# Two blocks of relation products kept in the tail of the row buffer, with nine own rows mixed a stage later

## The chip, the cores and the metric

The kernel runs on one core of a Trainium2 chip. The metric is device time in microseconds (us), the median over runs of the whole kernel. The engines are PE (TensorE: matmuls, with its weight loads shown as PEld), DVE (VectorE), ACT (ScalarE), POOL (GpSimd, which here issues the indirect gathers) and SP (SyncE, which issues plain loads).

## The reference, cut to what matters

A graph of 3125 nodes with 128 features and 53125 edges goes through four layers, each followed by a residual addition and a layer norm: ten steps of propagation, two graph-attention layers, one relational layer and one attention layer. The change lies where the second attention layer ends and the relational layer begins. The relational layer is this:

```python
out = x @ W0
h = jnp.einsum('nd,rdo->rno', x, W)          # 8 relations
msg = h[edge_type, src] * edge_weight[:, None]
out = out + jax.ops.segment_sum(msg, dst, num_segments=num_nodes)
return out / deg[:, None]                     # deg at least 1
```

So each node's row is multiplied by eight matrices (its relation products) and by W0 (its own product). Each edge then fetches one of the eight products of its source node, and the products are summed at the destination.

## The kernel before, in words

Nodes are cut into NB = 25 blocks of 128. Edges are sorted by destination and laid into tiles of 128 slots, CAP = 17 tiles for a block (7 for the last one). Blocks are grouped into seven SETS: 0 to 3, 4 to 7, 8 to 11, 12 to 15, 16 to 19, 20 to 21 and 22 to 24. All engines run one long program and meet only at semaphores; the order on each engine is written out by hand.

Second attention layer (`Layer`, followed by `IntoRelations`). For each block POOL gathers the edges' rows into `t.rows` (a ring of two blocks, 34 slots of 264 floats for each partition). DVE makes one-hot matrices, scores and messages, and PE sums the messages at the nodes. DVE's loop for block b begins with `at_nodes(b - 1)` and goes on with `raise_(b)` and `weigh(b)`, on whose results ACT's exponentials and PE's sums wait, then `messages(b)` and `close(b - 1)`. When a set is closed, DVE normalises it, PE applies `wo`, and DVE adds the result to x and normalises again (`IntoRelations.dve`). Some blocks later, at the places listed in `LATE`, PE multiplies two blocks by the nine relation matrices (L1924), ACT copies the eight relation products of each block to `t.stage` (L2027) and stores them from there to the table `rel_table_b`, and the own product goes to `t.own`.

`t.stage` has STAGES = 7 places, and block b uses place b % 7. DVE also needs the staged products: the loop edge of a node is not gathered but added by `mix(b)`, eight `scalar_tensor_tensor` (L1978) that add to `t.own` each of the eight products times a weight that is zero for all but the node's own relation. Block b + 7 may overwrite a place only when block b is stored (`tabled`) and mixed (`mixed`).

Before the change `MIXED_EARLY = NB - STAGES = 18`: blocks 0 to 17 are mixed inside the second attention layer, at the end of DVE's loop body, by `dve_mix`. Blocks 16 and 17 are mixed at the end of the body for block 22, directly ahead of `at_nodes(22)`. The other seven blocks (18 to 24) are mixed in the next stage, one for each of its first seven blocks. The last set, 22 to 24, has its products made at the very end, by `pe_last`, `act_last` and `dve_last` (L1933 and L1938 on PE, L1957 on ACT, L1970 on DVE, the stores at L1960). POOL waits for all 25 stores before the first gather of the relational layer (`Relations.pool`).

Relational layer (`Relations`). POOL issues 403 gathers (L2611) into `t.rows`, seen as a ring of REL_RING = 4 blocks of 17 rows of 128 floats. DVE makes weighted one-hots for the next block (L2645), mixes, and closes the block (L2651, L2653) when PE has summed it (L2632). After each set the products for the attention layer that follows are made (L2508, L2531, L2560 and the lines after it). Neighbouring blocks share one tile (`shared`, `fetched`): an odd block reads its first tile from the last slot of the even block ahead of it.

Of the kernel before, what the change touches and what calls it, by code (L numbers as in the profile page):

```python
# [16 lines left out]
P = 128  # L17
N = 3125
E = 53125
D = 128  # L20
NB = -(-N // P)
# [15 lines left out]
NREL = 8  # L37
# [6 lines left out]
CAP = 17  # L44
# [18 lines left out]
ALU = mybir.AluOpType  # L63
# [35 lines left out]
class Core:  # L99


    def __init__(self, nc, ctx, dram):
        self.nc, self.ctx, self.dram = nc, ctx, dram
        self.sems = []
# [18 lines left out]
def chained(eng, sem, start=0):  # L123


    count = [start]

    def then(ins):
        count[0] = count[0] + 1
        ins.then_inc(sem, 1)  # L130
        eng.wait_ge(sem, count[0])
    return then
# [1405 lines left out]


STAGES = 7  # L1540


class NormTiles:
# [46 lines left out]
class Tiles:  # L1590


    def __init__(self, c, ctx, y):
        def sb(name, shape, dt=f32):
            return c.sb(ctx, f"t_{name}", shape, dt)
# [29 lines left out]
        fresh = sb("fresh", [P, NB * (SPAN + 1) + 7], bf16)  # L1625
        stage = sb("stage", [P, STAGES, NREL * D])
        weights = sb("weights", [P, 2 * (F + 2 * HEADS)])
# [39 lines left out]
class Enter:  # L1667
# [32 lines left out]
    def pool(self, pool):  # L1700
        self.c.nc.gpsimd.iota(self.t.node[:, :], [[0, 1]], base=0, channel_multiplier=1, allow_small_or_imprecise_dtypes=True).then_inc(self.numbered, 1)
# [122 lines left out]
class IntoLayer:  # L1824
# [38 lines left out]
    def act_late(self, act, i, blocks):  # L1863
        pass
# [4 lines left out]
    def act_last(self, act):  # L1869
        pass  # L1870

    def dve_last(self, dve):
        pass
# [11 lines left out]
class IntoRelations:  # L1885
# [3 lines left out]
    def __init__(self, c, t, table):  # L1889
        self.c, self.t, self.table = c, t, table  # L1890
        self.early, self.late = 0, 0
        self.turned, self.copied, self.done, self.added, self.normed, self.step, self.x_turned, self.x_copied, self.x_done, self.x_out = (
            c.sem(f"into_rel_{n}") for n in ("turned", "copied", "products", "added", "normed", "step", "x_turned", "x_copied", "x_products", "x_out"))
        self.x_out_dve = c.sem("into_rel_x_out_dve")
        self.tabled = [c.sem(f"into_rel_tabled{q}") for q in range(STAGES)]
        self.mixed, self.mix_step = c.sem("into_rel_mixed"), c.sem("into_rel_mix_step")

    def pe(self, pe, layer, i):
        c, t, blocks = self.c, self.t, SETS[i]
# [46 lines left out]
    def act_last(self, act):  # L1946
        c, t, blocks = self.c, self.t, SETS[-1]
        n, k0, m = len(blocks), 3 * blocks[0], len(blocks) * P
        act.wait_ge(self.x_turned, len(SETS))
        act.wait_ge(self.x_done, k0)  # L1950
        c.nc.scalar.copy(t.turned_all[:, 0:m], t.pt[:, 0:m]).then_inc(self.x_copied, 1)
        rows = self.table.rearrange("(r n) f -> n r f", r=NREL)
        for j, b in enumerate(blocks):
            act.wait_ge(self.tabled[b % STAGES], 16 * (b // STAGES))
            act.wait_ge(self.mixed, b - STAGES + 1)
            act.wait_ge(self.x_done, k0 + 2 * j + 1)
            c.nc.scalar.copy(t.stage[:, b % STAGES, 0:4 * D], t.pr[0][:, 0:4 * D]).then_inc(self.x_out, 1)  # L1957
            act.wait_ge(self.x_out, k0 + j + 1)
            act.wait_ge(self.x_out_dve, j + 1)
            act.dma_start(rows[b * P:(b + 1) * P, :, :], t.stage[:, b % STAGES, :].rearrange("p (r f) -> p r f", r=NREL)).then_inc(self.tabled[b % STAGES], 16)  # L1960
        for j, b in enumerate(blocks):
            act.wait_ge(self.x_done, k0 + 2 * n + j + 1)
            c.nc.scalar.copy(t.own[:, b, 0:D], t.pr[j % 2][:, 0:D]).then_inc(self.x_out, 1)

    def dve_last(self, dve):
        t, blocks = self.t, SETS[-1]
        for j, b in enumerate(blocks):
            dve.wait_ge(self.tabled[b % STAGES], 16 * (b // STAGES))
            dve.wait_ge(self.x_done, 3 * blocks[0] + 2 * j + 2)
            self.c.nc.vector.tensor_copy(t.stage[:, b % STAGES, 4 * D:NREL * D], t.pr[1][:, 0:4 * D]).then_inc(self.x_out_dve, 1)  # L1970

    def mix(self, dve, b):

        c, t, v = self.c, self.t, self.c.nc.vector
        then = chained(dve, self.mix_step, b * NREL)
        total = t.own[:, b, 0:D]
        for r in range(NREL):
            last = v.scalar_tensor_tensor(total, t.stage[:, b % STAGES, r * D:(r + 1) * D], t.own_rel[:, r, b:b + 1], total, ALU.mult, ALU.add)  # L1978
            then(last)
        dve.nop().then_inc(self.mixed, 1)  # L1980

    def dve_mix(self, dve, blocks):
        for b in blocks:
            if b < MIXED_EARLY:
                dve.wait_ge(self.x_out, 3 * b + 3)
# [24 lines left out]
    def act_late(self, act, i, blocks):  # L2010
        c, t = self.c, self.t
        if blocks[0] == SETS[i][0]:
            m = len(SETS[i]) * P
            act.wait_ge(self.x_turned, i + 1)
            if i:
                act.wait_ge(self.x_done, 3 * blocks[0])
            c.nc.scalar.copy(t.turned_all[:, 0:m], t.pt[:, 0:m]).then_inc(self.x_copied, 1)
        rows = self.table.rearrange("(r n) f -> n r f", r=NREL)
        for b in blocks:
            if b >= STAGES:  # L2020
                act.wait_ge(self.tabled[b % STAGES], 16 * (b // STAGES))
                act.wait_ge(self.mixed, b - STAGES + 1)
            for n, (lo, hi) in enumerate(REL_PARTS):
                k = 3 * b + n
                act.wait_ge(self.x_done, k + 1)
                to = t.stage[:, b % STAGES, lo * D:hi * D] if n < 2 else t.own[:, b, 0:D]
                c.nc.scalar.copy(to, t.pr[k % 2][:, 0:(hi - lo) * D]).then_inc(self.x_out, 1)  # L2027
            act.wait_ge(self.x_out, 3 * b + 3)
            act.dma_start(rows[b * P:(b + 1) * P, :, :], t.stage[:, b % STAGES, :].rearrange("p (r f) -> p r f", r=NREL)).then_inc(self.tabled[b % STAGES], 16)

    def dve(self, dve, layer, i):
        c, t, blocks, v = self.c, self.t, SETS[i], self.c.nc.vector
# [11 lines left out]
for _i, _blocks in enumerate(SETS):  # L2044
    for _lo in range(0, len(_blocks), 2):
        LATE.setdefault(min(_blocks[-1] + 2 + _lo // 2, NB) if _blocks[-1] < NB - 4 else (NB - 1 if _blocks[-1] < NB - 1 else NB), []).append((_i, _blocks[_lo:_lo + 2]))
MIXED_EARLY = NB - STAGES
REL_PARTS = [(0, 4), (4, NREL), (NREL, NREL + 1)]
NORM_STEPS = 12

# [10 lines left out]
def fetched(b):  # L2061

    return tiles_of(b)[b % 2:]


def shared(b):

    return b % 2 == 0 and b < NB - 1
# [7 lines left out]
def arrived(b):  # L2076

    return 16 * sum(len(fetched(n)) for n in range(b % RING_BLOCKS, b + 1, RING_BLOCKS))
# [19 lines left out]
def slot(k):  # L2098
    return k % (RING_BLOCKS * CAP)
# [475 lines left out]
        last.then_inc(self.split, 1)  # L2575


REL_RING = 4


class Relations:
# [3 lines left out]
    def __init__(self, c, t, table, before, after):  # L2585
        self.c, self.t, self.table, self.before, self.after = c, t, table, before, after
        self.tabled = before.tabled
        self.step, self.hot, self.summed, self.freed, self.normed = (c.sem(f"relations_{n}") for n in ("step", "hot", "summed", "freed", "normed"))
        self.gathered = [c.sem(f"relations_gathered{q}") for q in range(REL_RING)]
        self.rows = t.rows[:, :, :].rearrange("p s f -> p (s f)")[:, 0:REL_RING * CAP * D].rearrange("p (s f) -> p s f", f=D)  # L2590
        self.gathered_last = c.sem("relations_gathered_last")
        self.first_lot = len(tiles_of(NB - 1)) - 2

    def slot(self, k):
        return k % (REL_RING * CAP)

    def arrived(self, b):
        return 16 * sum(len(fetched(n)) for n in range(b % REL_RING, b + 1, REL_RING))

    def pool(self, pool):  # L2600
        c, t = self.c, self.t
        for q, tabled in enumerate(self.tabled):
            pool.wait_ge(tabled, 16 * len(range(q, NB, STAGES)))
        for b in range(NB):
            for k in fetched(b):
                if b >= REL_RING and (k % CAP % SUM_GROUP == 0 or k == fetched(b)[0]):
                    pool.wait_ge(self.summed, groups_through(k - REL_RING * CAP))
                if b >= REL_RING and k == (b + 1) * CAP - 1 and shared(b):
                    pool.wait_ge(self.summed, groups_through((b + 1 - REL_RING) * CAP))
                landed = self.gathered_last if k >= (NB - 1) * CAP + self.first_lot else self.gathered[b % REL_RING]  # L2610
                c.nc.gpsimd.indirect_dma_start(self.rows[:, self.slot(k), :], None, self.table,  # L2611
                                               bass.IndirectOffsetOnAxis(ap=t.rel[:, k:k + 1], axis=0)).then_inc(landed, 16)
# [24 lines left out]
    def dve(self, dve, own_out):  # L2637
# [20 lines left out]
        for b in range(NB):  # L2658
            if b + 1 < NB:
                make_hots(b + 1)  # L2660
            if b == 0:
                dve.wait_ge(*own_out)
            if b < NB - MIXED_EARLY:
                self.before.mix(dve, MIXED_EARLY + b)
            if b - 1 in SET_DONE:
# [1314 lines left out]
```

## Time and profile before

| | us |
|---|---|
| median of 3 runs | 3375.05 |
| lowest and highest of them | 3374.46, 3377.92 |
| the profiled execution, its own time | 3375.13 |
| its span in the profile | 3373.5 |
| second attention layer's last gather starts | 2212.95 |
| first gather of the relational layer starts | 2272.46 |
| last gather of the relational layer starts | 2778.94 |

Places in the trace are given in us from the start of the span. A row of a timeline gives start, duration, engine, line, operation and operands, the count of merged instructions, and in brackets how long the engine had been idle and what ended that. The granted clock of PE stands as 1.0 for full speed (2.4 GHz) and 0.5 for half (1.2 GHz).

### The profile page before, as it was taken

To read this page: it belongs to the slowest core of one execution; us is meant where nothing else is said; L and a number is where in the kernel's file an instruction comes from. 1 tells how busy PE (TensorE), PEld (TensorE's weight loads), DVE (VectorE), ACT (ScalarE), POOL (GpSimd) and SP (SyncE) were. 2 spreads that over 40 slices of the span, in tenths; PEclk is the share of its full clock that TensorE was granted. 3 is DMA by queue.
4 is the path that set the end of the run, shared out by engine and by line. 5 is a ranking of instruction groups with operands and counts; after the bars stand their busy time and mean duration, and the time that the engine had idled before them with its cause. 6 is when DMAs were issued, how large, how long until landed. Compare 5 with 4: busy or idle time off the path is not lost.

```text
span 3373.5 us, 42846 instructions
## 1 busy us (share of the span) xinstructions
PE 2122.9 (63%) x14275; PEld 1837.1 (54%) x14276; DVE 2171.8 (64%) x5824; ACT 1245.3 (37%) x1339; POOL 1821.5 (54%) x1791
## 2 busy tenths in 40 slices
PE   2875999999999255666546666652333343555455
PEld 1554999999998244444434444432333333554444
DVE  7997777767768177666747888873433335555555
ACT  1986667666765223333233333320000002222222
POOL 3333222222221377777477777727777776777771
PEclk7987999999999577777767777776666666666667
DMA  2100000000000444444255555422222223444441
GB/s 63 24 1 1 0 0 0 0 0 0 0 0 15 149 129 140 139 139 135 78 153 154 145 145 148 138 88 53 59 59 58 59 61 117 132 132 132 133 123 38
DMA packets 133665, 264.99 MB, mean 79 GB/s; under 512 B 33930, under 2 KB 77558, under 8 KB 133446
## 3 DMA queue, kind: packets, MB, share of 16 engines
q0 software_dynamic: 72208, 188.45, 20.6%
q1 hardware_dynamic: 24614, 50.78, 4.7%
q10 hardware_dynamic: 36692, 23.93, 2.2%
q8 instruction: 72, 1.18, 0.1%
q14 instruction: 79, 0.65, 0.1%
HBM read 235.41 MB, written 27.85 MB: 78 GB/s over the span
## 4 chain that ended last, share of the span: by engine, by line
POOL 32%; DVE 13%; issue 12%; PE 8%; DMA 2%; ACT 1%; ACTq 1%; POOLq 0%; DVEq 0%
POOL t_rows L2190 12%; POOL t_rows L2611 11%; POOL t_rows L2945 9%; DVE t_rows L2390 3%; PE t_sum_ps L2298 2%; DVE t_own L1978 2%; DVE t_onehot L2117 1%; PE t_product_ps L1924 1%; ACTq L1821 1%; PE t_sum_ps L3005 1%; PE t_sum_ps L2632 1%; DMA t_rows<-kv_table_b,t_src 0%; PE t_small_ps L2984 0%; DVE t_stage L3029 0%; DVE t_so_far L2361 0%
## 5 line engine op out<-in xcount | busy, mean ns | idle before, releaser
L2190 POOL DMA_INDIRECT t_rows<-gat_table,t_src x806 | 770.9, 956 | 354.1 <-issue 242.5
L1238 PE MATMUL hop_ps<-parts,wide 128*128 128x256 f32 x5900 | 713.8, 284 | 4.0 <-DVE parts L1334 2.8
L1238 PEld LDWEIGHTS hop_ps<-parts,wide 128*128 128x128 f32 x5900 | 711.2, 192 | 6.0 <-issue 3.5
L1289 ACT CAST wide<-counts 128x3200 fp32r<-128x3200 fp8e4 x177 | 506.2, 2863 | 230.9 <-PE hop_ps L1238 211.3
L2298 PE MATMUL t_sum_ps<-t_rows,t_onehot 128*128 128x264 f32 x1660 | 468.9, 451 | 101.7 <-DVE t_rows L2390 101.7
L2611 POOL DMA_INDIRECT t_rows<-rel_table_b,t_rel x403 | 385.0, 955 | 181.0 <-issue 180.1
L1299 POOL CAST wide<-counts 128x3200 fp32r<-128x3200 fp8e4 x59 | 168.7, 2859 | 580.7 <-PE hop_ps L1238 564.6
L2298 PEld LDWEIGHTS t_sum_ps<-t_rows,t_onehot 128*128 128x128 f32 x1660 | 372.1, 228 | 182.3 <-issue 104.8
L2945 POOL DMA_INDIRECT t_rows<-kv_table_b,t_src x403 | 384.1, 953 | 137.1 <-issue 120.9
L2632 PE MATMUL t_sum_ps<-t_rows,t_onehot 128*128 128x128 f32 x830 | 147.2, 360 | 295.1 <-DMA t_rows<-rel_table_b,t_rel 295.1
L2632 PEld LDWEIGHTS t_sum_ps<-t_rows,t_onehot 128*128 128x128 f32 x830 | 143.0, 272 | 303.9 <-issue 301.3
L2984 PE MATMUL t_small_ps<-t_own,t_turned 128*128 128x128 bf16 x957 | 110.8, 312 | 255.1 <-DVE t_stage L3029 250.0
L2390 DVE TENSOR_TENSOR t_rows<-t_rows,t_sum_ps 128x768 f32<-128x768 f32 (+1 forms) x288 | 251.7, 903 | 15.4 <-ACT t_sum_ps L2228 15.4
L2984 PEld LDWEIGHTS t_small_ps<-t_own,t_turned 128*128 128x128 bf16 x957 | 97.9, 146 | 269.8 <-DVE t_stage L3029 264.5
L2651 DVE TENSOR_TENSOR t_own<-t_own,t_sum_ps 128x128 f32<-128x128 f32 x25 | 7.2, 288 | 305.4 <-PE t_sum_ps L2632 305.4
L2117 DVE TENSOR_TENSOR t_onehot<-t_small_ps,t_dst 128x768 f32<-128x768 f32 (+1 forms) x222 | 194.9, 898 | 0.2
L1076 PE MATMUL cnt_ps<-hot_column,hot_src 128*128 128x320 bf16 x830 | 161.3, 336 | 45.6 <-DVE hot_column L1121 36.0
L3029 DVE TENSOR_TENSOR t_stage<-t_rows,t_small_ps 128x512 f32<-128x512 f32 x98 | 55.4, 587 | 196.3 <-DMA t_rows<-kv_table_b,t_src 191.3
L2520 ACT COPY t_turned_all<-t_turn_ps 128x512 f32<-128x512 f32 (+2 forms) x7 | 3.8, 540 | 477.1 <-PE t_turn_ps L2500 477.1
L2150 ACT ACTIVATE t_apart<-t_dst_wide,t_node 128x2176 f16<-128x2176 f16 (+1 forms) x75 | 153.9, 2051 | 20.9 <-DMA t_dst_wide<-dst_row 20.6
L2154 ACT ACTIVATE t_turned<-t_apart,ones 128x2176 bf16<-128x2176 f16 (+1 forms) x75 | 154.9, 2066 | 2.5
L1076 PEld LDWEIGHTS cnt_ps<-hot_column,hot_src 128*128 128x128 bf16 x830 | 99.7, 147 | 98.1 <-issue 55.9
(452 smaller groups left out, 3332.0 us busy)
## 6 DMA issues: line engine op xcount, KB each, us to landing
t_dst_wide<-dst_row SPq DMA_DIRECT2D x72, 544.0 KB, 4.1
t_rows<-gat_table,t_src POOLq DMA_INDIRECT x806, 2.9
rel_table_b<-t_stage ACTq DMA_DIRECT2D x25, 512.0 KB, 3.3
t_rows<-rel_table_b,t_rel POOLq DMA_INDIRECT x403, 2.5
t_rows<-kv_table_b,t_src POOLq DMA_INDIRECT x403, 2.8
gat_table<-t_own ACTq DMA_DIRECT2D x10, 520.0 KB, 5.2
kv_table_b<-t_fresh ACTq DMA_DIRECT2D x5, 512.0 KB, 2.9
out<-x SPq DMA_DIRECT2D x6, 256.0 KB
```

The source lines that it names most:

```text
L1076: last = nc.tensor.matmul(bank[:, h * 512:h * 512 + JH], hot_src[:, g % 2, :, n], hot[:, k % RING, h * JH:(h + 1) * JH], start=(k == ks[0] ...
L1238: last = nc.tensor.matmul(ps[bank][0:columns.shape[-1], 0:2 * D], columns[:, k, :], parts[old][:, k, :], start=(k == 0), stop=(k == NB - 1))
L1289: nc.scalar.copy(wide[b % B][:, :, :], column(b)).then_inc(widened, 1)
L1299: nc.gpsimd.tensor_copy(wide[B - 1][:, :, :], column(b)).then_inc(pool_widened, 1)
L2117: last = v.tensor_tensor(t.onehot[:, hot_at(ks[lo]):hot_at(ks[lo]) + m, :], t.iota.rearrange("p (o d) -> p o d", o=1).to_broadcast([P, m, P]),
L2190: c.nc.gpsimd.indirect_dma_start(t.rows[:, slot(k), 0:FW], None, self.table, bass.IndirectOffsetOnAxis(ap=t.src[:, k:k + 1], axis=0)).then ...
L2298: product = c.nc.tensor.matmul(t.pa[b % 2][:, 0:RW], t.onehot[:, hot_at(k), :], t.rows[:, slot(k), :], start=(n == 0), stop=(n == len(ks) ...
L2390: v.tensor_tensor(h, h, self.weight(b)[:, tiles[0]:tiles[0] + m, :].rearrange("p t (h o) -> p t h o", o=1).to_broadcast([P, m, HEADS, HID] ...
L2611: c.nc.gpsimd.indirect_dma_start(self.rows[:, self.slot(k), :], None, self.table, bass.IndirectOffsetOnAxis(ap=t.rel[:, k:k + 1], axis=0)) ...
L2632: product = c.nc.tensor.matmul(t.pa[b % 2][:, 0:D], t.onehot[:, hot_at(k), :], self.rows[:, self.slot(k - (k not in fetched(b))), :], star ...
L2945: c.nc.gpsimd.indirect_dma_start(t.rows[:, slot(k), 0:2 * D], None, self.table, bass.IndirectOffsetOnAxis(ap=t.src[:, k:k + 1], axis=0)).t ...
L2984: last = c.nc.tensor.matmul(self.looked_ps[j][:, m * P:(m + 1) * P], t.turned[:, b % 2, n * P:(n + 1) * P], query[:, i, :], start=(i == 0) ...
```

## The change

The relation products of the last two blocks, 23 and 24, no longer go to `t.stage` but to a `spare` area: the part of `t.rows` behind the ring of the relational layer, which shrinks from four blocks to three to make room. So places 2 and 3 of `t.stage` keep the products of blocks 16 and 17, and these two need not be mixed before the last set is staged. `MIXED_EARLY` falls from 18 to 16, and the relational layer mixes nine blocks (16 to 24), one for each of its first nine. For blocks 23 and 24 the waits on `tabled` and `mixed` are left out. With an odd ring the condition for the reuse of a shared slot moves from `shared(b)` to `shared(b - REL_RING)`.

```diff
+SPARE_STAGES = 2
...
+        at = REL_RING * CAP * D
+        self.spare = t.rows[:, :, :].rearrange("p s f -> p (s f)")[:, at:at + SPARE_STAGES * NREL * D].rearrange("p (s f) -> p s f", s=SPARE_STAGES)
+
+    def staged(self, b):
+
+        if b >= NB - SPARE_STAGES:
+            return self.spare[:, b - (NB - SPARE_STAGES), :]
+        return self.t.stage[:, b % STAGES, :]
...
         for j, b in enumerate(blocks):
-            act.wait_ge(self.tabled[b % STAGES], 16 * (b // STAGES))
-            act.wait_ge(self.mixed, b - STAGES + 1)
+            if b < NB - SPARE_STAGES:
+                act.wait_ge(self.tabled[b % STAGES], 16 * (b // STAGES))
+                act.wait_ge(self.mixed, b - STAGES + 1)
             act.wait_ge(self.x_done, k0 + 2 * j + 1)
-            c.nc.scalar.copy(t.stage[:, b % STAGES, 0:4 * D], t.pr[0][:, 0:4 * D]).then_inc(self.x_out, 1)
+            c.nc.scalar.copy(self.staged(b)[:, 0:4 * D], t.pr[0][:, 0:4 * D]).then_inc(self.x_out, 1)
...
-            dve.wait_ge(self.tabled[b % STAGES], 16 * (b // STAGES))
+            if b < NB - SPARE_STAGES:
+                dve.wait_ge(self.tabled[b % STAGES], 16 * (b // STAGES))
...
-            last = v.scalar_tensor_tensor(total, t.stage[:, b % STAGES, r * D:(r + 1) * D], t.own_rel[:, r, b:b + 1], total, ALU.mult, ALU.add)
+            last = v.scalar_tensor_tensor(total, self.staged(b)[:, r * D:(r + 1) * D], t.own_rel[:, r, b:b + 1], total, ALU.mult, ALU.add)
...
-MIXED_EARLY = NB - STAGES
+MIXED_EARLY = NB - STAGES - SPARE_STAGES
...
-REL_RING = 4
+REL_RING = 3
...
-                if b >= REL_RING and k == (b + 1) * CAP - 1 and shared(b):
+                if b >= REL_RING and k == (b + 1) * CAP - 1 and shared(b - REL_RING):
                     pool.wait_ge(self.summed, groups_through((b + 1 - REL_RING) * CAP))
```

The remaining lines of the diff put `self.staged(b)` where `t.stage[:, b % STAGES, :]` stood, for the stores and for `dve_last`.

## Rows read from the trace of the kernel before

**Rows 1.** The page: span, busy shares, and the chain by engine and line

```profile
span 3373.5 us, 42846 instructions
PE 2122.9 (63%) x14275; PEld 1837.1 (54%) x14276; DVE 2171.8 (64%) x5824; ACT 1245.3 (37%) x1339; POOL 1821.5 (54%) x1791
POOL 32%; DVE 13%; issue 12%; PE 8%; DMA 2%; ACT 1%; ACTq 1%; POOLq 0%; DVEq 0%
```

**Rows 2.** The chain in order of time, 2212 to 2273: start, us, what

```profile
2212.80 0.35 DVE x L1586
2213.16 0.03 issue
2213.18 0.36 DVE t_own L1978
...
2219.10 0.36 DVE t_own L1978
...
2219.67 0.23 DVE t_own_l L2396
...
2223.70 0.97 DVE t_rows L2390
...
2224.80 6.85 PE t_sum_ps L2298 x18
...
2243.69 3.69 PE t_product_ps L1924 x4
...
2248.05 2.00 PE t_product_ps L1924 x4
...
2268.09 3.36 DMA rel_table_b<-t_stage
...
2271.55 0.04 POOLq L2603
2271.59 0.04 issue
```

**Rows 3.** Timeline of DVE where no mix follows the second norm

```profile
2169.92 1.14 DVE L1586 TENSOR_SCALAR x<-x,t_norm_both,t_norm_pair 128x128 f32<-128x128 f32 x4
2171.10 0.22 DVE L2396 SCALAR_TENSOR_TENSOR t_own_l<-t_sum_ps,alone,t_own_e 128x4 f32<-128x4 f32 x1
```

**Rows 4.** Timeline of PE, ACT and POOL from 2208 to 2225

```profile
2209.05 0.68 PE L2268 MATMUL t_small_ps<-ident,t_es 128*68 128x64 f32 x6
2212.95 1.01 POOL L2190 DMA_INDIRECT t_rows<-gat_table,t_src  x1 [0.30 <-issue]
2221.39 0.38 PE L2276 MATMUL t_small_ps<-ident,t_highest 68*128 68x68 f32 x1 [11.66 <-DVE t_highest L2363]
2223.29 0.26 ACT L2227 ACTIVATE t_rows<-t_logit 128x68 f32<-128x68 f32 x1 [14.79 <-DVE t_logit L2377]
2224.89 0.20 ACT L2216 COPY t_es<-t_rows 128x28 f32<-128x28 f32 x1
```

**Rows 5.** The page: the second attention layer's gathers, issue to landing

```profile
t_rows<-gat_table,t_src POOLq DMA_INDIRECT x806, 2.9
```

**Rows 6.** Windows: length, busy us of PE, PEld, DVE, ACT, POOL, clock, DMA

```profile
2214.00:2219.00 5.00, 0.00 (x0) 0.00 (x0) 4.46 (x13) 0.00 (x0) 0.00 (x0) 0.50 0.12 27
2228.00:2231.70 3.70, 3.70 (x15) 2.99 (x14) 3.49 (x9) 0.00 (x0) 0.00 (x0) 0.72 0.00 0
2243.69:2247.40 3.71, 3.71 (x6) 1.64 (x6) 3.32 (x17) 0.59 (x1) 0.00 (x0) 0.54 0.00 0
2248.05:2250.05 2.00, 2.00 (x5) 0.80 (x6) 1.60 (x6) 0.70 (x2) 0.00 (x0) 1.00 0.41 134
```

**Rows 7.** Groups by line, 2272 to 2800: busy, mean ns, idle before

```profile
L2611 POOL DMA_INDIRECT t_rows<-rel_table_b,t_rel x403 | 385.0, 955 | 181.0 <-issue 180.1 <-PE t_sum_ps L2632 0.9
L1978 DVE SCALAR_TENSOR_TENSOR t_own<-t_stage,t_own_rel,t_own 128x128 f32<-128x128 f32 x56 | 19.7, 352 | 1.7
L2651 DVE TENSOR_TENSOR t_own<-t_own,t_sum_ps 128x128 f32<-128x128 f32 x25 | 7.2, 288 | 305.4 <-PE t_sum_ps L2632 305.4
```

**Rows 8.** Timeline of DVE, relational layer's blocks 1 and 8

```profile
2305.89 3.05 DVE L1978 SCALAR_TENSOR_TENSOR t_own<-t_stage,t_own_rel,t_own 128x128 f32<-128x128 f32 x8
2459.72 0.69 DVE L2560 TENSOR_TENSOR t_own_prod<-t_fresh 128x512 f32<-128x512 f32 x1 [3.19 <-ACT t_fresh L2531]
```

**Rows 9.** Timeline of POOL: gathers with and without a mix beside them

```profile
2306.38 1.06 POOL L2611 DMA_INDIRECT t_rows<-rel_table_b,t_rel  x1 [0.30 <-issue]
2307.75 0.94 POOL L2611 DMA_INDIRECT t_rows<-rel_table_b,t_rel  x1 [0.30 <-issue]
2308.99 0.94 POOL L2611 DMA_INDIRECT t_rows<-rel_table_b,t_rel  x1 [0.30 <-issue]
```

**Rows 10.** Timeline of PE: the sums of blocks 0 and 8

```profile
2295.30 5.48 PE L2632 MATMUL t_sum_ps<-t_rows,t_onehot 128*128 128x128 f32 x34 [26.00 <-DMA t_rows<-rel_table_b,t_rel]
2461.34 5.66 PE L2632 MATMUL t_sum_ps<-t_rows,t_onehot 128*128 128x128 f32 x34 [2.18 <-DMA t_rows<-rel_table_b,t_rel]
```

More of the change, by code:

```diff
@@ L1953, in act_last @@
         for j, b in enumerate(blocks):
-            act.wait_ge(self.tabled[b % STAGES], 16 * (b // STAGES))
-            act.wait_ge(self.mixed, b - STAGES + 1)
+            if b < NB - SPARE_STAGES:
+                act.wait_ge(self.tabled[b % STAGES], 16 * (b // STAGES))
+                act.wait_ge(self.mixed, b - STAGES + 1)
             act.wait_ge(self.x_done, k0 + 2 * j + 1)
-            c.nc.scalar.copy(t.stage[:, b % STAGES, 0:4 * D], t.pr[0][:, 0:4 * D]).then_inc(self.x_out, 1)
+            c.nc.scalar.copy(self.staged(b)[:, 0:4 * D], t.pr[0][:, 0:4 * D]).then_inc(self.x_out, 1)
             act.wait_ge(self.x_out, k0 + j + 1)
             act.wait_ge(self.x_out_dve, j + 1)
-            act.dma_start(rows[b * P:(b + 1) * P, :, :], t.stage[:, b % STAGES, :].rearrange("p (r f) -> p r f", r=NREL)).then_inc(self.tabled[b % STAGES], 16)
+            act.dma_start(rows[b * P:(b + 1) * P, :, :], self.staged(b).rearrange("p (r f) -> p r f", r=NREL)).then_inc(self.tabled[b % STAGES], 16)
         for j, b in enumerate(blocks):
@@ L1967, in dve_last @@
         for j, b in enumerate(blocks):
-            dve.wait_ge(self.tabled[b % STAGES], 16 * (b // STAGES))
+            if b < NB - SPARE_STAGES:
+                dve.wait_ge(self.tabled[b % STAGES], 16 * (b // STAGES))
             dve.wait_ge(self.x_done, 3 * blocks[0] + 2 * j + 2)
-            self.c.nc.vector.tensor_copy(t.stage[:, b % STAGES, 4 * D:NREL * D], t.pr[1][:, 0:4 * D]).then_inc(self.x_out_dve, 1)
+            self.c.nc.vector.tensor_copy(self.staged(b)[:, 4 * D:NREL * D], t.pr[1][:, 0:4 * D]).then_inc(self.x_out_dve, 1)
     def mix(self, dve, b):
@@ L2025, in act_late @@
                 act.wait_ge(self.x_done, k + 1)
-                to = t.stage[:, b % STAGES, lo * D:hi * D] if n < 2 else t.own[:, b, 0:D]
+                to = self.staged(b)[:, lo * D:hi * D] if n < 2 else t.own[:, b, 0:D]
                 c.nc.scalar.copy(to, t.pr[k % 2][:, 0:(hi - lo) * D]).then_inc(self.x_out, 1)
             act.wait_ge(self.x_out, 3 * b + 3)
-            act.dma_start(rows[b * P:(b + 1) * P, :, :], t.stage[:, b % STAGES, :].rearrange("p (r f) -> p r f", r=NREL)).then_inc(self.tabled[b % STAGES], 16)
+            act.dma_start(rows[b * P:(b + 1) * P, :, :], self.staged(b).rearrange("p (r f) -> p r f", r=NREL)).then_inc(self.tabled[b % STAGES], 16)
     def dve(self, dve, layer, i):
```

## The prediction

> **What bounds the kernel now.** I read the page first. No engine is busy for more than two thirds of the span, and the chain that ended last is mostly gathers issued by POOL, with DVE second [rows 1]. The shares of a whole span don't price an edit, so I went to the place that the change touches. The next view was the chain in order of time from 2212 to 2273, the joint between the second attention layer and the relational layer. There the reader should see that all sixteen mixes of blocks 16 and 17 lie on the chain, back to back from 2213.18, after DVE's second norm and ahead of `at_nodes` at 2219.67. From there it goes over DVE, ACT and PE to the last store of the table, and POOL's first gather starts at 2272.46 when that has landed [rows 2]. Then I read the timeline of the other engines over the same stretch, to see whether one of them would be the next to hold the chain, and last the groups and timelines of the relational layer, which receives the moved mixes. In that layer POOL never waits for work: of 181.0 us of idle time before its gathers 180.1 are its own issue gaps (58.5 of them the gap before the first), and 0.9 is put to PE [rows 7]. Its 402 steps from 2272.46 to 2778.94 take 1.26 us each. DVE by contrast waits 305.4 us for PE's sums, some 12 us for each of 25 blocks [rows 7].
>
> **What is removed.** Blocks 16 and 17 lose 2 x 8 = 16 mixes at the end of DVE's body for block 22. The place of removal is priced by its own rows: the first mix starts at 2213.18 and the instruction after the last at 2219.67, which is 6.49 us [rows 2]. What would follow the norm instead is `at_nodes`. The trace has that transition one set earlier, where nothing is mixed: the norm's last group ends at 2169.92 + 1.14 = 2171.06 and `at_nodes` starts at 2171.10, 0.04 later [rows 3]. Here the norm ends at 2213.15, so `at_nodes` would start near 2213.19. Removed: 6.48 us.
>
> Does this pass through? Four things could be late next. PE's layout of the scores for block 23 ended at 2209.73, before the removed stretch, and PE then idled 11.66 us until DVE had its running maximum [rows 4]. ACT idled 14.79 us before the exponentials of block 23 and waited for DVE [rows 4]; moved up by 6.5 it still has 8.3. POOL's last gather of this layer starts at 2212.95 and takes 1.01 [rows 4]; with the 2.9 from issue to landing [rows 5] the rows of block 24 are there at about 2216.9, counted from the end of the issue. ACT reads them at 2224.89 [rows 4], which becomes 2218.4: a margin of 1.5 us, and the result of that read is not used by PE until after half of block 23's sums. And `at_nodes(22)` needs the sums of block 22, which lie well before. So I take the whole 6.5 as passing through. The bounds are nothing (if some wait that the trace hides stands at 2219) and 6.5.
>
> **What the removed waits give.** ACT loses two waits for each of blocks 23 and 24, DVE one for each. They stand ahead of waits for PE's products that come later anyway. A wait that passes shows as 0.04 on a queue, with the same again between two (POOL's at L2603) [rows 2], so six are worth 0.5 us at most if nothing hid them; I take nothing.
>
> **What is moved to the relational layer.** It mixes nine blocks, not seven. Each mix is 8 instructions in 3.05 us [rows 8]. The two added ones fall to its blocks 7 and 8. The average idle time there is 12 us for a block; the tightest is block 8, where the set of blocks 4 to 7 is also prepared for the next layer: DVE sat idle for 3.19 us ahead of L2560 [rows 8], just enough for 3.05. If a few tenths stick out, they delay work that is needed 300 us later. On DVE the added 6.1 us therefore cost nothing; uncovered they would cost 6.1.
>
> POOL is the engine that sets this layer's end, so what a mix does to a gather counts. Beside the mix at 2305.89 one gather took 1.06 in place of 0.94, and its step was 1.37, against 1.24 for the next [rows 8, 9]. One such gather for a mix is what I see, about 0.12 us; two more mixes make 0.2 us. The bounds are nothing and the full duration of the sixteen, 16 x 0.352 = 5.6 us [rows 7]. The Trainium skill speaks against the change here: "GPSIMD Engine Reference", section 1 (Specifications), says that GpSimd's SBUF interfaces are shared with VectorE and that instructions with two SBUF inputs contend; a mix has two. By that rule, taken at its strongest, the sum would lose 5.6; by the row it loses 0.2. The trace agrees that there is an effect, but with a thirtieth of that size, so the sum goes by the row.
>
> **The ring of three.** Before the first gather of block b POOL now needs the sums of block b - 3. Between the last gather of block b - 3 and the first of b lie two blocks, 33 x 1.26 = 41.6 us. Block 0's sums ended at 2300.78, about 7 us after its 17 gathers (2272.46 + 17 x 1.26 = 2293.9) [rows 2, 10]. Block 8, with a set's work ahead of it on PE, still waited 2.18 us for its gathers before it summed for 5.66 [rows 10]. So 34 us of slack are left, and the ring costs nothing. Block 3 has four waits that it hadn't (three groups and one shared slot); at 0.08 each [rows 2] that is 0.3 us at most, and I take nothing, as the gaps between gathers are 0.30 for all [rows 9]. The store of blocks 23 and 24 from another tile has the same shape and size, so I leave 3.36 [rows 2] as it is.
>
> **The sum.** It is made against the profiled execution, 3375.13 us, which is 0.08 above the median. 3375.13 - 6.48 + 0.2 = 3368.85, and on the median's scale 3368.8.
>
> **The clock.** PE idles through the removed stretch at a granted 0.50, and after it the steps of the clock lie inside work that is on the chain: it rises within 2228.0 to 2231.7 (mean 0.72), and four matmuls of L1924 take 3.69 us at 0.54 where the next four take 2.00 at 1.00 [rows 2, 6]. If the moved program meets the steps elsewhere, one such group more at half speed costs 1.69 us, and one fewer gives 1.69 us. The rows don't say which, and the sum takes neither. The Trainium skill, "TensorE: Matmul & The Clock Gate", section "What's actually happening", says that the monitor behind the clock runs freely and isn't reset at a kernel's start; by that the two cases would come and go from run to run. No row here shows it.
>
> **Rivals.**
> 1. The forecast, 3368.8: the stretch passes through, the clock is neutral. Chance 0.55. With the spread of the unchanged kernel's runs (-0.6 to +2.9 about the median) some four tenths of it end beyond the 0.2% bound.
> 2. A clock step falls well: 3368.8 - 1.7 = 3367.1. For it: 3.69 against 2.00. Chance 0.21.
> 3. A clock step falls badly: 3368.8 + 1.7 = 3370.5. Chance 0.16.
> 4. The stretch is covered by something that the chain doesn't show, for instance the last gathers landing late: nothing is saved, 3375.1 + 0.2 = 3375.3. Against it: the four margins above. Chance 0.03.
> 5. POOL's gathers stand still for as long as each moved mix lasts: 3368.8 - 0.2 + 5.6 = 3374.2. Against it: one step of 1.37, where the 3.05 us of a mix would have to be added [rows 8, 9]. Chance 0.02. The page "GPSIMD Engine Reference" of the Trainium skill, section 1, is what could bring it about.
> 6. The other side: the ring of three stalls POOL. It decides once POOL's stalls add up to more than 6.3 us, or 0.29 us for each of the 22 blocks from 3 to 24. If each were to wait only 1 us, 22 us would come on top: 3390.8. For it, each block's sums would have to end over 34 us later than they do. Chance 0.03.
>
> A change of 0.2%, 6.75 us, is about what a measurement of this kernel can tell from none, so "faster" means under 3368.3. My forecast lies half a microsecond on the near side of that line. Faster: 0.55 x 0.4 + 0.21 = 0.43. Slower: 0.03. The same: 0.54. The range holds cases 1 to 3 with the spread of runs: 3366.0 to 3371.8.
>
> **What the profile after would show.** No L1978 between the norm's L1586 and L2396 of block 22, and a gap of 0.04 there. The first gather of the relational layer near 2266.0 in place of 2272.46, with 58.5 - 6.5 = 52 us before it. L1978 x72 in the relational layer; POOL's steps still 1.26 us, its first to last gather 506.5 to 506.9. POOL's waits for PE still about 1 us. DVE idle before L2651 some 6 us less. The prediction is wrong if the first gather comes less than 5 us earlier (step "passes through"), if first to last gather grows by over 1 us (mixes on gathers, or the ring), or if the gain at 2266 is given back after 2780, where I expect nothing to change.

## The result and the profile after

The changed kernel takes 3367.94 us (median of 9 runs, 3363.90 to 3370.51), beside 3375.10 for the kernel before on the same chip (9 runs, 3374.23 to 3377.92). The ratio is 0.9976 with a 95% interval of 0.9966 to 0.9987. Two more meetings on other chips gave 0.9984 (0.9975 to 0.9993) and 0.9978 (0.9969 to 0.9987). So it is faster by 5 to 8 us by the ratios (by 6.0 to 8.1 by the medians); 6.3 were forecast.

The chain in order of time of the changed kernel, at the place of [rows 2] (line numbers are 11 higher in this kernel from the relational classes on, so L2396 is now L2407, L1978 is L1989 and L2611 is L2622):

```profile
2212.19 0.39 DVE x L1587
2212.58 0.02 issue
2212.60 0.23 DVE t_own_l L2407
...
2217.72 6.60 PE t_sum_ps L2309 x18
...
2236.36 3.58 PE t_product_ps L1933 x4
...
2240.60 2.00 PE t_product_ps L1933 x4
...
2260.45 2.92 DMA rel_table_b<-t_rows
```

No mix stands between the norm and `at_nodes` any more, and the gap is the 0.02 us that was to be seen. Behind it everything has moved up. The timeline of the same kernel, at the places of [rows 4] and the first two gathers of the relational layer:

```profile
2214.31 0.37 PE L2287 MATMUL t_small_ps<-ident,t_highest 68*128 68x68 f32 x1 [4.85 <-DVE t_highest L2374]
2216.21 0.26 ACT L2238 ACTIVATE t_rows<-t_logit 128x68 f32<-128x68 f32 x1 [8.95 <-DVE t_logit L2388]
2217.81 0.20 ACT L2227 COPY t_es<-t_rows 128x28 f32<-128x28 f32 x1
2264.37 0.97 POOL L2622 DMA_INDIRECT t_rows<-rel_table_b,t_rel  x1 [51.92 <-issue]
2265.65 0.98 POOL L2622 DMA_INDIRECT t_rows<-rel_table_b,t_rel  x1 [0.30 <-issue]
```

PE and ACT still wait for DVE, PE for 4.85 us where it was 11.66 and ACT for 8.95 where it was 14.79. Neither has become what is late next. The first gather starts at 2264.37, not 2272.46; POOL's gap ahead of it shrank from 58.50 to 51.92 us. That is 8.1 us earlier, where 6.5 were forecast.

Counted from the end of the second norm to that first gather, the stretch fell from 59.31 us (2213.15 to 2272.46, [rows 2]) to 51.79 (2212.58 to 2264.37). Of these 7.5 us 6.50 are the mixes. Most of the rest lies behind them on the same chain: the last store took 2.92 us for 3.36, one group of sums 6.60 for 6.85, the first group of products 3.58 for 3.69. The table below counts from the attention layer's last gather instead, and so finds 6.6: that gather starts 1.08 us before the norm's end here, and 0.20 before it in the kernel before.

The groups by line of the relational layer, after, beside [rows 7]:

```profile
L2622 POOL DMA_INDIRECT t_rows<-rel_table_b,t_rel x403 | 385.8, 957 | 174.4 <-issue 172.9 <-PE t_sum_ps L2643 1.5
```

POOL waits 1.5 us for PE, against 0.9: the ring of three is not felt. The layer's first to last gather takes 507.3 us, a little over the 506.5 to 506.9 that were expected.

A kernel of this length is best compared stage by stage between gathers. In this table "layer" is the second attention layer from its first to its last gather, "joint" runs from there to the relational layer's first gather, "relational" is that layer's first to last gather, and "mixed" says how many blocks are mixed early and late. Each number is the difference of two starts in that kernel's profile, one execution each. The changed kernel's second profile was taken on the chip of mixes back, mixes left out and four spare; its third on the chip of four spare again and the last two. Ring only, 16 more mixes and one mix a body had no changed kernel beside them on their chip.

| kernel | mixed | ring | layer | joint | relational | ratio (95% interval) |
|---|---|---|---|---|---|---|
| before | 18 / 7 | 4 | 529.0 | 59.5 | 506.5 | |
| changed | 16 / 9 | 3 | 528.5 | 52.9 | 507.3 | 0.9976 (0.9966 to 0.9987) |
| changed, second | 16 / 9 | 3 | 530.7 | 53.4 | 507.5 | 0.9984 (0.9975 to 0.9993) |
| changed, third | 16 / 9 | 3 | 528.8 | 52.2 | 505.9 | 0.9978 (0.9969 to 0.9987) |
| mixes back | 18 / 7 | 3 | 529.1 | 58.9 | 506.9 | 1.0004 (0.9995 to 1.0013) |
| mixes left out | 16 / 7 | 4 | 528.7 | 53.0 | 506.2 | 0.9985 (0.9976 to 0.9994) |
| ring only | 18 / 7 | 3 | 528.9 | 59.7 | 505.8 | 0.9999 (0.9990 to 1.0008) |
| 16 more mixes | 16 / 9 + 16 | 3 | 528.8 | 52.1 | 506.8 | 0.9981 (0.9972 to 0.9990) |
| four spare | 14 / 11 | 2 | 525.7 | 52.2 | 508.2 | 0.9973 (0.9964 to 0.9982) |
| four spare, again | 14 / 11 | 2 | 526.0 | 52.1 | 506.5 | 0.9969 (0.9957 to 0.9981) |
| one mix a body | 16 / 9 | 3 | 532.5 | 52.1 | 506.2 | 0.9991 (0.9982 to 1.0000) |
| mix in the wait | 16 / 9 | 3 | 523.7 | 53.6 | 506.0 | 0.9963 (0.9949 to 0.9976) |
| mix in the wait, four spare | 14 / 11 | 2 | 523.9 | 50.9 | 506.3 | 0.9951 (0.9937 to 0.9965) |

### The profile page after: what moved, and what is told of

The parts are those of the page before. It is cut to its first block, busy times and chain, and to the rows that moved or that the text cites. A ratio compares the mean times of both kernels' runs of the same rounds, so it can differ in the third digit from the quotient of the medians.

```text
span 3366.0 us, 42841 instructions
## 1 busy us (share of the span) xinstructions
PE 2126.3 (63%) x14275; PEld 1841.2 (55%) x14276; DVE 2169.8 (64%) x5824; ACT 1245.1 (37%) x1339; POOL 1822.0 (54%) x1791
## 4 chain that ended last, share of the span: by engine, by line
POOL 32%; DVE 13%; issue 12%; PE 7%; DMA 2%; ACT 1%; ACTq 1%; POOLq 0%; DVEq 0%
POOL t_rows L2201 12%; POOL t_rows L2622 11%; POOL t_rows L2956 9%; DVE t_rows L2401 3%; PE t_sum_ps L2309 2%; DVE t_own L1989 1%; DVE t_onehot L2128 1%; PE t_product_ps L1933 1%; ACTq L1822 1%; PE t_sum_ps L2643 1%; PE t_sum_ps L3016 1%; DMA t_rows<-kv_table_b,t_src 0%; DVE t_stage L3040 0%; PE t_small_ps L2995 0%; DVE t_so_far L2372 0%
## 5 line engine op out<-in xcount | busy, mean ns | idle before, releaser
L1289 ACT CAST wide<-counts 128x3200 fp32r<-128x3200 fp8e4 x177 | 506.3, 2863 | 230.9 <-PE hop_ps L1238 211.3
L2622 POOL DMA_INDIRECT t_rows<-rel_table_b,t_rel x403 | 385.8, 957 | 174.4 <-issue 172.9
L2662 DVE TENSOR_TENSOR t_own<-t_own,t_sum_ps 128x128 f32<-128x128 f32 x25 | 7.2, 288 | 303.5 <-PE t_sum_ps L2643 303.5
```

The source lines that it names most:

```text
L1289: nc.scalar.copy(wide[b % B][:, :, :], column(b)).then_inc(widened, 1)
```

## The experiments

**Mixes back.** The changed kernel with one line turned back:

```diff
-MIXED_EARLY = NB - STAGES - SPARE_STAGES
+MIXED_EARLY = NB - STAGES
```

> The changed kernel (spare area, ring of three) with the mixes of blocks 16 and 17 put back where they were, inside the second attention layer. Theory (the gain is the sixteen mixes taken off the chain, nothing else): the time of the kernel before, 3375 us within 1 us, ratio 1.000, and the first gather of the relational layer back at about 2272. Rival (the gain comes from the left-out waits or from the store out of the other tile): it stays near 3368.

Measured 3377.44 us beside 3376.50, ratio 1.0004. The spare area, the waits left out and the ring of three are all in this kernel and bring nothing that shows in the time. Its chain has the mixes where they were, and its first gather is back (the second fence is its timeline of POOL):

```profile
2213.37 0.36 DVE t_own L1989
...
2219.86 0.23 DVE t_own_l L2407
```

```profile
2272.10 0.94 POOL L2622 DMA_INDIRECT t_rows<-rel_table_b,t_rel  x1 [57.95 <-issue]
```

From first mix to `at_nodes` it is 2219.86 - 2213.37 = 6.49 us, the same as in [rows 2] to the hundredth.

**Mixes left out.** The kernel before, with the mixes of blocks 16 and 17 in nobody's hands, so that its output lacks them (cut to the main lines):

```diff
-        then = chained(dve, self.mix_step, b * NREL)
+        then = chained(dve, self.mix_step, (b if b < 16 else b - 2) * NREL)
...
                 dve.wait_ge(self.x_out, 3 * b + 3)
-                self.mix(dve, b)
+                if b < 16:
+                    self.mix(dve, b)
+                else:
+                    dve.nop().then_inc(self.mixed, 1)
```

> The kernel before with the sixteen mixes of blocks 16 and 17 left out altogether, so that the own relation products of these two blocks are missing from the output; ring of four, no spare area. Theory: 6.5 us less than before, 3368.6, first gather at about 2266. Against the changed kernel it shows what the moved mixes and the ring cost: theory 0.2 us, rival (POOL held while DVE mixes) up to 5.6 us, so that this kernel would be that much faster than the changed one.

Measured 3371.70 us, ratio 0.9985, where the changed kernel beside it had 0.9984. The joint is 53.0 us. Leaving the work out and moving it are worth the same within the intervals, about 3 us each way. The comparison isn't quite clean: this kernel's last store takes 3.60 us against 2.92 of the changed one, and its step from the norm to `at_nodes` 0.37 against 0.03, so up to 1 us of cost could hide in it. The rival of 5.6 us falls.

**Ring only.** The kernel before with `REL_RING = 3` and `shared(b - REL_RING)`.

> The kernel before with nothing but the ring of three in the relational layer (and its condition on the shared slot). Theory: no change, 1.000 within the interval, first to last gather of the relational layer 506.5 to 507.0 us, POOL's waits for PE under 3 us. Rival (the ring is what lengthened that layer from 506.5 to 507.3 in the changed kernel): 507.2 or more here, with seven mixes in it.

Measured 3375.15 beside 3374.65, ratio 0.9999, and 505.8 us for the relational layer. The ring costs nothing, and the 0.8 us by which that layer was longer in the changed kernel's first profile is not the ring's either.

**Sixteen more mixes.** In `Relations.dve` of the changed kernel:

```diff
+            else:
+                scratch = t.seen[:, 0, 0:16, :].rearrange("p a b -> p (a b)")
+                for r in range(NREL):
+                    again(v.scalar_tensor_tensor(scratch, t.stage[:, 3, r * D:(r + 1) * D], t.own_rel[:, r, b:b + 1], scratch, ALU.mult, ALU.add))
```

> The changed kernel with eight more instructions of the mix's form, on a scratch tile, for each of the relational layer's blocks 9 to 24: 128 more, 45 us of DVE time. They change no output. By the prediction's row (0.12 us for a mix) the layer's first to last gather grows by 1.9 us and the time by as much; by what the changed kernel's own layer showed (0.8 us more for two mixes, the ring included) by up to 6.4 us; by the rule that POOL stands still while DVE reads two operands from SBUF, by 45 us.

Measured 3368.66 us, ratio 0.9981. The groups by line of the relational layer, in the order of the columns of [rows 7], and POOL's and DVE's timelines round one of the added mixes:

```profile
L2623 POOL DMA_INDIRECT t_rows<-rel_table_b,t_rel x403 | 385.3, 956 | 173.6 <-issue 172.7 <-PE t_sum_ps L2644 0.9
L2681 DVE SCALAR_TENSOR_TENSOR t_seen<-t_stage,t_own_rel,t_seen 128x128 f32<-128x128 f32 x128 | 45.2, 353 | 4.0
```

```profile
2464.54 1.00 POOL L2623 DMA_INDIRECT t_rows<-rel_table_b,t_rel  x1 [0.30 <-issue]
2465.85 0.94 POOL L2623 DMA_INDIRECT t_rows<-rel_table_b,t_rel  x1 [0.30 <-issue]
2467.09 0.94 POOL L2623 DMA_INDIRECT t_rows<-rel_table_b,t_rel  x1 [0.30 <-issue]
```

```profile
2465.07 3.12 DVE L2681 SCALAR_TENSOR_TENSOR t_seen<-t_stage,t_own_rel,t_seen 128x128 f32<-128x128 f32 x8
```

45.2 us of added DVE work with two operands from SBUF stand beside gathers, and all 403 gathers together take 385.3 us, against 385.8 without it. The layer is 506.8 us long. The 45 us and the 6.4 us fall by that. The 1.9 us do not show in the layer either, but its length scatters by as much between profiles of one kernel (505.9 to 507.5 for the changed one), so this has to be looked at gather by gather. The two gathers above that start inside the mix take 0.94 us, as most do. Others don't; here is one, and the added mix beside it:

```profile
2698.40 1.21 POOL L2623 DMA_INDIRECT t_rows<-rel_table_b,t_rel  x1 [0.30 <-issue]
2698.44 3.06 DVE L2681 SCALAR_TENSOR_TENSOR t_seen<-t_stage,t_own_rel,t_seen 128x128 f32<-128x128 f32 x8
```

In this kernel's trace 41 gathers overlap an added mix by more than 0.3 us and have no mix beside them in the profiles of the change, of one mix a body and of mix in the wait. Here they take 0.976 us on average; in those five profiles the same 41 take 0.952 to 0.969, mean 0.957. That makes some 0.7 us for sixteen mixes, an estimate from these means: about 0.05 us for a mix, not 0.12.

**Four spare places.** The change taken twice as far, with a guard that `act_late` then needs:

```diff
-SPARE_STAGES = 2
+SPARE_STAGES = 4
-            if b >= STAGES:
+            if STAGES <= b < NB - SPARE_STAGES:
-REL_RING = 3
+REL_RING = 2
```

> The change taken twice as far: four blocks (21 to 24) staged in the tail, ring of two, mixes of blocks 14 and 15 moved out of the second attention layer too, so that the relational layer mixes eleven blocks. If each sixteen mixes are worth their full length wherever they stand: another 6.3 us, 3361.6. My theory: at that place the gathers of block 20 land 2.6 us before the mixes end, so only these 2.6 us are to be had, less 0.2 for mixes beside gathers: 3365.5. Rival (a ring of two stalls POOL): slower than the changed kernel, by a microsecond or more for each block.

Measured 3369.09 us beside 3370.48 for the changed kernel, ratios 0.9973 and 0.9984. The intervals overlap, so it went again, with the changed kernel beside it again:

> The kernel with four spare places and a ring of two, once more, beside the changed kernel on the same chip. If its joint and layer times hold: 3 us less than the changed kernel. Rival (the 1.4 us between the medians was chance): the same within 1 us.

This time it was 3365.17 beside 3366.88, ratios 0.9969 and 0.9978. Both pairs say less, by 1.4 and 1.7 us in the medians and by 3.7 and 3.0 in the ratios (0.0011 and 0.0009 of 3375), which neither settles alone; the stages do. Of what was expected, the full 6.3 us and the stalled ring fall, and the 2.4 of the theory fit. The layer takes 525.7 and 526.0 us against 528.5, 530.7 and 528.8, and a ring of two doesn't stall POOL (its waits for PE in the relational layer are 1.5 and 2.1 us in the two profiles). DVE's timeline of the four-spare kernel shows why sixteen mixes brought 6.5 us at one place and half of that here:

```profile
2136.58 0.22 DVE L2407 SCALAR_TENSOR_TENSOR t_own_l<-t_sum_ps,alone,t_own_e 128x4 f32<-128x4 f32 x1 [0.59 <-PE t_sum_ps L2309]
2140.28 0.55 DVE L2372 TENSOR_TENSOR_SCAN t_so_far<-t_fresh,t_small_ps 68x192 f32<-68x192 bf16 x1 [3.28 <-PE t_small_ps L2279]
```

With the mixes of blocks 14 and 15 gone DVE comes to `raise_` early and idles 3.28 us for PE, which lays out scores that have only just been gathered (in the changed kernel sixteen mixes stand here, from 2135.01 on, and neither of the two waits is there). The second four-spare profile has 2.87 us at the same place. Part of the removed work turned into waiting.

**One mix a body.** In `Layer.dve` of the changed kernel:

```diff
-            for _, blocks in LATE.get(b - 1, []):
-                self.after.dve_mix(dve, blocks)
+            if b >= 6:
+                self.after.dve_mix(dve, [b - 6])
```

> The changed kernel with the sixteen early mixes spread: block b - 6 is mixed in DVE's body for block b, one for each of bodies 6 to 21, in place of two in each of eight bodies. Theory (a mix on DVE costs only what sticks out of DVE's waits for gathers and sums, and POOL's waits for PE, 25 us in this layer, are DVE's lateness handed on): a body without mixes has 2.8 us of idle time ahead of at_nodes, one in four, so some 2.8 us for each of the four sets of four blocks that have mixes, 8 to 12 us less than the changed kernel. Rival (the chain counts each mix in full wherever it stands): no change.

Measured 3372.03 us, ratio 0.9991: the 8 to 12 us of the theory miss, and it looks slower than the changed kernel, though its interval (0.9982 to 1.0000) overlaps those of that kernel a little. The stages say more: the layer grew from 528.5 to 532.5 us (530.7 and 528.8 in the changed kernel's other two profiles), so the rival's "no change" misses too. The waits of POOL in that layer, first of this kernel and then of the changed one (us in total, times, longest):

```profile
POOL t_rows L2201 <- PE t_sum_ps L2309: 28.9, 10, 6.7
```

```profile
POOL t_rows L2201 <- PE t_sum_ps L2309: 25.0, 7, 5.9
```

The 3.9 us that POOL waits longer are the 4.0 by which the layer grew. This holds for all thirteen profiles of the table: the layer less these waits of POOL for PE is 503.1 to 504.1 us in every one, so what makes this layer longer or shorter is these waits. DVE's timeline of the spread kernel points to the mixes that did it:

```profile
2044.45 3.05 DVE L1989 SCALAR_TENSOR_TENSOR t_own<-t_stage,t_own_rel,t_own 128x128 f32<-128x128 f32 x8
2047.72 0.22 DVE L2407 SCALAR_TENSOR_TENSOR t_own_l<-t_sum_ps,alone,t_own_e 128x4 f32<-128x4 f32 x1 [0.21 <-DVE t_own L1989]
2052.20 0.55 DVE L2372 TENSOR_TENSOR_SCAN t_so_far<-t_fresh,t_small_ps 68x192 f32<-68x192 bf16 x1 [4.06 <-PE t_small_ps L2279]
...
2078.54 3.06 DVE L1989 SCALAR_TENSOR_TENSOR t_own<-t_stage,t_own_rel,t_own 128x128 f32<-128x128 f32 x8
2081.82 0.22 DVE L2407 SCALAR_TENSOR_TENSOR t_own_l<-t_sum_ps,alone,t_own_e 128x4 f32<-128x4 f32 x1 [0.21 <-DVE t_own L1989]
```

The mix at 2044.45 is followed by 4.06 us of waiting for the gathers' scores: at least one more would have been free there, as it was in the order of the changed kernel. The one at 2078.54 stands at the end of a body that has just closed a set and normed twice, where DVE comes straight to `at_nodes` without a wait. That such a mix is the costly kind is a reading so far; the next kernel tests it.

**Mix in the wait.** From that reading, the mix of the four set-closing bodies moves up by one step, in front of the second norm:

```diff
             view(b + 1)
+            if b >= 6 and b - 1 in SET_DONE:
+                self.after.dve_mix(dve, [b - 6])
             if b - 1 in SET_DONE:
                 self.after.dve(dve, self, SET_DONE[b - 1])
...
-            if b >= 6:
+            if b >= 6 and b - 1 not in SET_DONE:
                 self.after.dve_mix(dve, [b - 6])
```

> As the kernel with one mix a body, but in the four bodies that close a set (8, 12, 16, 20) the mix stands in front of the second norm, where DVE idles 3.1 us for PE's products of wo, and not behind it. Theory (what counts is whether a mix falls into a wait of DVE's): the second attention layer's first to last gather falls from 532.5 us to some 520, 8 us under the changed kernel's 528.5, and the time with it: 0.995 to 0.996 of the kernel before. Rival (a mix costs 3.1 us wherever it stands): 532 again. Rival (the gathers take over as the bound): between 524 and 528.

Measured 3363.49 us beside 3374.98, ratio 0.9963. The changed kernel beside it had 3366.88 and 0.9978: 3.4 us less by the medians, 5 by the ratios, with intervals that overlap a little (0.9949 to 0.9976 and 0.9969 to 0.9987). First the changed kernel's timeline of DVE at that place, then this kernel's:

```profile
2075.54 0.69 DVE L2047 TENSOR_TENSOR x<-x,t_turn_ps 128x512 f32<-128x512 f32 x1 [3.13 <-PE t_turn_ps L1919]
```

```profile
2071.90 3.06 DVE L1989 SCALAR_TENSOR_TENSOR t_own<-t_stage,t_own_rel,t_own 128x128 f32<-128x128 f32 x8
2075.10 0.69 DVE L2047 TENSOR_TENSOR x<-x,t_turn_ps 128x512 f32<-128x512 f32 x1
```

The mix fills what was a wait of 3.13 us, and L2047 starts as soon as before. The layer takes 523.7 us, 8.8 less than with one mix a body and 4.8 less than changed. The 520 of the theory were not reached; 523.7 is just outside the 524 to 528 of the rival that the gathers take over as the bound, so that rival may be part of it. POOL's waits for PE in this layer are down to 19.7 us:

```profile
POOL t_rows L2201 <- PE t_sum_ps L2309: 19.7, 8, 4.5
```

**Both together.** The same edit on the kernel with four spare places:

> The same placing of the mixes on the kernel with four spare places and a ring of two: fourteen blocks are mixed early, one in each of bodies 6 to 19, eleven late. Theory: as the kernel with the mix in the wait, or up to 3 us less, as bodies 20 and 21 mix nothing: 0.994 to 0.996 of the kernel before. Rival: the mixes of those two bodies cost nothing there, no difference.

Measured 3359.36 us, ratio 0.9951 (0.9937 to 0.9965). This version beats both kernels, by some 16 us the kernel before and by 7.5 (medians) to 9 (ratios) the changed one. Against the mix in the wait alone its layer is no shorter (523.9 against 523.7) and its joint is (50.9 against 53.6); the two intervals overlap, so that step alone isn't settled. The shorter joint is in good part a matter of PE's clock. First this kernel's timeline of PE at the first products behind the sums, then the changed kernel's, and the granted clock of either stretch (the number before the last two of its row):

```profile
2232.82 2.37 PE L1933 MATMUL t_product_ps<-t_w_rel,t_turned_all 128*128 128x512 f32 x6 [2.95 <-ACT t_turned_all L2028]
2236.36 3.79 PE L1933 MATMUL t_product_ps<-t_w_rel,t_turned_all 128*128 128x512 f32 x6 [2.95 <-ACT t_turned_all L2028]
```

```profile
2232.82:2235.19 2.37, 2.36 (x6) 0.97 (x6) 2.20 (x10) 0.94 (x2) 0.00 (x0) 1.00 0.00 0
2236.36:2240.15 3.79, 3.79 (x6) 1.65 (x6) 3.38 (x18) 0.78 (x2) 0.00 (x0) 0.58 0.00 0
```

The same six matmuls took 1.42 us less at a granted 1.00, and this group has left the chain. That is the prediction's second rival, a clock step that falls well, seen in this one profile of thirteen.

**The change, second and third time.** They are the partners of the others on their chips.

> The changed kernel itself, unchanged, for a comparison on the same chip as the others and for its spread. Theory: 3368 to 3369; its runs spread over some 6 us as PE's clock steps fall on or off the chain. Rival: the spread seen so far was chance and they lie within 3 us.

> The changed kernel itself, a third time, as the partner of the other three on this chip: 0.998 of the kernel before.

Measured 3370.48 us (3368.34 to 3374.99, 11 runs) and 3366.88 (3363.19 to 3369.63, 11 runs). The first is over the 3368 to 3369 that were expected. The spread of 6.6 us is there, but it is not the change's: the kernel before spread from 3373.32 to 3381.36 in the 33 runs beside the first of the two. The changed kernel's three profiles, of executions between 3363.19 and 3371.99 us, differ by only 0.11 us in the products at this place (3.58, 3.69, 3.63), so the clock there isn't what spread those three.

## Why the prediction was right, point by point

**What bounds the kernel at the joint: right, shown.** The sixteen mixes were on the chain. Taken out, moved or put back they are worth 6 to 7 us of the joint: 59.5, 59.7 and 58.9 us with them (mean 59.4), 52.9, 53.4, 52.2, 53.0 and 52.1 without them (the three profiles of the change, mixes left out, 16 more mixes; mean 52.7). That is 6.7 where the term of the sum was 6.48, and in the changed kernel's own rows the step from the norm to `at_nodes` fell from 6.52 to 0.02, by the 6.5 itself. None of the four margins became the bound. ACT read block 24's scores at 2217.81; the last gather had started at 2211.50, and with the same duration and landing as before its rows were there near 2215.4.

**The removed waits and the ring at nothing: right, shown** by the two kernels that have the one or both without the move of the mixes, at 0.9999 and 1.0004.

**The last store left at 3.36 us: mis-sized by 0.44.** The prediction took same size and same shape for same time. The store took 2.92 us, and this gain is not in the sum. It helped to bring the measured 3367.94 under the forecast 3368.8; with the other scatter of the stages below it makes the closeness of the two in part luck.

**DVE's cover in the relational layer: right, but not where I put it.** I expected 6 us less idle time ahead of the close of a block. It fell from 305.4 to 303.5, because at most block 7's mix came out of that wait. Block 8's came out of the wait ahead of L2560, 3.19 us in [rows 8] and here, in the same view of the changed kernel, 0.39:

```profile
2448.54 3.05 DVE L1989 SCALAR_TENSOR_TENSOR t_own<-t_rows,t_own_rel,t_own 128x128 f32<-128x128 f32 x8
2451.98 0.69 DVE L2571 TENSOR_TENSOR t_own_prod<-t_fresh 128x512 f32<-128x512 f32 x1 [0.39 <-ACT t_fresh L2542]
```

**Mixes beside gathers at 0.2 us: right in kind, about twice too large.** I took one gather of 1.06 us in [rows 9] for what every mix does. It is rarer than that. In the trace of before 17 gathers overlap a mix by more than 0.3 us. They take 0.974 us on average, the 380 that overlap none 0.954, and only four of the 17 take over 1.0. The gathers beside a mix are the slower ones in each of the thirteen profiles, by 0.006 to 0.037 us in the mean. At the 0.05 us for a mix that the sixteen added ones give, two cost some 0.1 us, which no total can show: all 403 gathers take 384.3 to 386.6 us over the thirteen profiles, and the layer 505.8 to 508.2 without following the number of mixes closely (7: 505.8 to 506.9; 9: 505.9 to 507.5; 11: 506.3 to 508.2; 25: 506.8). The Trainium skill states contention of GpSimd with VectorE instructions that have two SBUF inputs, in "GPSIMD Engine Reference", section 1 (Specifications). The trace agrees that there is some, and not that a gather stands still for as long as the instruction: beside 45.2 us of them 41 gathers lost some 0.7 us together. That takes away the prediction's bound of 5.6 us and its fifth rival.

**The clock: neither rival came in the changed kernel, and one came elsewhere.** Both were made of one group of four matmuls (L1924, now L1933) at the other speed, 1.69 us. In twelve of the thirteen profiles this group is on the chain, took 3.46 to 3.69 us there, and the next group 2.00 in all of them. So although the mixes moved the work by 6.5 us, the steps of PE's clock lay within some tenths of a microsecond of the same work. In the thirteenth, mix in the wait with four spare places, the group ran at full speed, as the rows above show. By twelve profiles the chances that I gave the two, 0.21 and 0.16, look too high; by the thirteenth the cause was a real one. That the monitor behind the clock runs freely, as the Trainium skill has it in "TensorE: Matmul & The Clock Gate", section "What's actually happening", would let the steps wander between executions of one kernel. The three profiles of the changed kernel do not show it, and the thirteenth can't tell it from the effect of another order of the work. What spreads the runs is open.

**The half microsecond on which "faster" hung.** The forecast was 3368.8, the bound 3368.3, the median 3367.94. On another chip the ratio was 0.9984, on the far side of the 0.2%, so on which side a measurement falls is chance, as the prediction had it. Between the two profiles some 7.5 us of span went as follows: 0.9 earlier at the layer's start and 0.6 in the layer, where nothing was changed; 6.6 in the joint; 0.8 given back in the relational layer; 0.1, -0.4 and 0.6 in the three stretches behind it. Of these only the joint, and 0.1 of what the relational layer gave back, can be put to the change. The other differences are no larger than those between the three profiles of the changed kernel (up to 2.4 us at the layer's start, 2.2 in the layer, 1.6 in the relational layer).

## What to carry to other kernels

Price work that leaves a chain by the start-to-start of its own rows, and check that the other engines arrive earlier than the moved time; do it place by place, since the same sixteen instructions were worth 6.5 us in one body and some 3 in another. An order written by hand should put side work into the waits of its engine: the same four mixes cost over 8 us more behind the second norm of a set than in front of it, and that placement gave more than the buffer that the change was about. One slow instruction beside a suspect is not a rate. Add many suspects, and compare the same instructions with and without one beside them: the total was blind to an effect that this shows.

## What the runs showed of the hardware that I had not expected

The last store of the table landed sooner from the tail of `t.rows` than from `t.stage`, with the same 512 KB and the same shape. From `t.stage` it took 3.36, 3.54 and 3.60 us (before, ring only, mixes left out), from the tail 2.91 to 2.92 in eight profiles, 3.05 with the mixes back and 3.10 with one mix a body. In the changed kernel's own profile the median store takes 3.3 us from `t.stage` (23 stores) and 2.9 from the tail (2 stores). That is 0.3 to 0.7 us on the chain. Ring only and mixes back come nearest to parting the causes: both mix 18 blocks early and have a ring of three, and they differ in the place of the last two blocks' products and the waits left out for them. They have 3.54 and 3.05 us. So it points to the place in SBUF, by one profile each, and not to the mixes; why the place should matter, no run shows.
